# Delta-rule attention: the triangular inverse in 64 by 64 blocks on two array tiles, and the corner block made once

## What is computed

```python
def step(Sm, inp):
    q_, k_, v_, g_, b_ = inp
    Sm = Sm * jnp.exp(g_)[..., None, None]
    kv = jnp.einsum('bhk,bhkv->bhv', k_, Sm)
    delta = (v_ - kv) * b_[..., None]
    Sm = Sm + jnp.einsum('bhk,bhv->bhkv', k_, delta)
    o = jnp.einsum('bhk,bhkv->bhv', q_, Sm)
    return (Sm, o)
_, o = jax.lax.scan(step, S0, (qt, kt, vt, gt, bt))
...
og = o * jax.nn.silu(z)
var = jnp.mean(og * og, axis=-1, keepdims=True)
on = og * jax.lax.rsqrt(var + EPS) * norm_w
return on.reshape(B, S, VAL_DIM) @ w_out
```

## Time and profile before

| | us |
|---|---|
| median of three runs | 6048.98 (6040.39 to 6051.36) |
| span of the profiled execution | 6046.2 |
| delta loop with its last block, in that span | 3160.4 |
| busy in the span: PE / DVE / ACT / POOL | 5221.5 / 3480.2 / 3055.8 / 1178.3 |
| mean granted clock of TensorE over the span | 0.930 |

### The profile page before, as it was taken

One profiled execution on the slowest core, in us unless ns is written; L12 is line 12 of the kernel. 1 busy time (PEld: TensorE's weight loads), 2 busy tenths in 40 slices (PEclk: granted clock), 3 DMA queues, 4 the chain that ended last, 5 costly groups with the idle time before them and its releaser, 6 DMA issues. The chain is left out here.

```text
span 6046.2 us, 91895 instructions
## 1 busy us (share of the span) xinstructions
PE 5221.5 (86%) x32318; PEld 3893.8 (64%) x32318; DVE 3480.2 (58%) x6531; ACT 3055.8 (51%) x8923; POOL 1178.3 (19%) x1352
## 2 busy tenths in 40 slices
PE   5799999999989999989999699899998597399969
PEld 4477777877877778877887555555555354255545
DVE  3466666676666667666766566555552554543331
ACT  2466666666656666666666344344441244325421
POOL 0222222322222222222232100011110321002210
PEclk7799999999999999999999799899999798688879
DMA  2000000000000000000000100100000100000000
GB/s 85 19 19 17 13 19 19 18 17 17 19 19 13 17 19 19 17 14 19 22 19 13 46 1 1 65 1 0 0 0 20 27 1 13 21 1 1 1 21 14
DMA packets 51094, 103.57 MB, mean 17 GB/s; under 512 B 12848, under 2 KB 20176, under 8 KB 49520
## 3 DMA queue, kind: packets, MB, share of 16 engines
q1 hardware_dynamic: 50672, 98.07, 5.4%
HBM read 90.43 MB, written 5.52 MB: 16 GB/s over the span
## 5 line engine op out<-in xcount | busy, mean ns | idle before, releaser
L896 ACT ACTIVATE dh_pb<-bank 64x128 f32<-64x128 f32 x3072 | 831.4, 271 | 272.5 <-PE bank L670 239.3
L684 PE MATMUL bank<-dh_cw,dh_pb 128*128 128x128 f32 x5120 | 701.5, 281 | 113.0 <-ACT dh_pb L896 111.4
L684 PEld LDWEIGHTS bank<-dh_cw,dh_pb 128*128 128x128 f32 x5120 | 635.5, 193 | 191.1 <-ACT dh_pb L896 164.4
L1034 DVE SCALAR_TENSOR_TENSOR dh_kq<-bank,dh_conv_kq,dh_kq 128x511 f32<-128x511 f32 (+2 forms) x408 | 305.4, 749 | 184.8 <-ACT dh_kq L853 173.6
L902 ACT ACTIVATE dh_cw<-bank 128x256 f32<-128x256 f32 x640 | 244.9, 385 | 255.1 <-PE bank L684 247.9
L621 PE MATMUL bank<-hT,dh_w_kq 128*128 128x512 f32 x544 | 276.7, 633 | 83.2 <-DVE dh_kq L1034 75.3
L1034 DVE SCALAR_TENSOR_TENSOR dh_v<-bank,dh_conv_v,dh_v 128x511 f32<-128x511 f32 (+2 forms) x384 | 284.2, 747 | 91.3 <-ACT dh_v L853 82.2
L1797 PE MATMUL bank<-moe_h_split,moe_w 128*128 128x512 bf16 x1200 | 277.1, 381 | 14.6 <-PEq L89 14.6
L633 PE MATMUL bank<-dh_w_vz,hT 128*128 128x256 f32 x1024 | 245.5, 383 | 22.0 <-ACT dh_zs L864 22.0
L1128 DVE TENSOR_TENSOR dh_zz<-dh_zz,bank 128x512 f32<-128x512 f32 x130 | 89.2, 686 | 283.0 <-PE bank L597 281.1
L621 PE MATMUL bank<-hT,dh_w_vz 128*128 128x512 f32 x512 | 242.5, 596 | 8.6 <-DVE dh_v L1034 8.6
(11 more groups left out here) (416 smaller groups left out, 12170.8 us busy)
## 6 DMA issues: line engine op xcount, KB each, us to landing
dh_rates<-delta_rates SPq DMA_DIRECT2D x130, 256.0 KB, 3.6
dh_w_vz<-in_L_wvz SPq DMA_DIRECT2D x17, 512.0 KB, 3.3
mod_w<-in_L_wmod SPq DMA_DIRECT2D x4, 1536.0 KB, 7.0
dh_w_kq<-in_L_wkq SPq DMA_DIRECT2D x18, 256.0 KB, 2.6
dh_wo<-in_L_wo SPq DMA_DIRECT2D x16, 256.0 KB, 4.2
moe_w<-in_L_w13T SPq DMA_DIRECT2D x1, 3200.0 KB, 15.7
later_gates<-mod_gate SPq DMA_DIRECT2D x3, 1024.0 KB, 4.0
gate<-later_gates SPq DMA_DIRECT2D x6, 512.0 KB, 3.4
```

The lines of the kernel that those rows point to most:

```text
L684: last = pe.matmul(square(j)[:, b, :, :], pb[j][:, b, :], src[:, :, b, :], start=True, stop=True)
L896: last = act.activation(out[half, :, o, half], src[halves[o], :, half], ACT.Copy)
L1034: dve.scalar_tensor_tensor(y, pj_bank(n)[:, 0:S - i], taps(n)[:, TAPS - 1 - i:TAPS - i], y, ALU.mult, ALU.add).then_inc(s["v_cs" if i < TA ...
```

## The change

The powers now live in 64 by 64 tiles of the array. Each of the two diagonal blocks of a matrix has its own tile: rows 0 to 63 of the array with columns 0 to 63, and rows 64 to 127 with columns 64 to 127. Calls alternate between the two tiles, then between heads, then sequences. Both a power and its transpose are carried along, so that nothing is transposed in the steps: `flip` turns the first power by a product with the identity; `next_power` (five times) makes the next power from the two; `next_turned` (five) makes the next turned power and the next summand of the turned sum; `inverse` makes the last factor's product, in both orders. The corner block of the inverse is then made once, by `corner_left` (on the tile from the first rows to the last columns) and `corner` (back), and stands in `ttb`. With it `z_prod` alone solves the system: `w_prod`, `w_copy`, `x_prod` and `zeta` are gone. On ACT, `keep_power`, `keep_turned`, `first_block`, `diagonal`, `left_copy` and `corner_copy` take the place of `power` and `power_c`; `qk_copy` on ACT copies k q^T without a mask in place of `qk_mask` on DVE. On DVE, `grow` stays, `last_factor` (L1146) is new, `inverse` and `zeta` are gone.

All recurrence products now share one bank a head (`R_BANK`), where before `B_AUX` was a third. The order of the stages is written anew on PE, ACT and DVE; on POOL `off_diagonal` waits for `corner_left` of the stage before and no longer for w.

```diff
+    def flip(pe, t):
+        for j in HEADS:
+            after(pe, hs[j]["v_u"], t)
+            after(pe, hs[j]["a_u12"], t)
+            for b in range(NB):
+                for p in halves:
+                    last = pe.matmul(pow_bank(j)[p, b, :], c0[j][p, b, :], turn[j][p, EYE, b, :], start=True, stop=True)
...
-        for b in range(NB):
-            last = pe.matmul(square(j)[:, b, :, :], pb[j][:, b, :], src[:, :, b, :], start=True, stop=True)
+        for b in range(NB):
+            for j in HEADS:
+                for p in range(2):
+                    last = pe.matmul(pow_bank(j)[target(j, p), b, :], turn[j][halves[p], CT, b, :], power(i, j)[halves[p], b, :],
+                                     start=True, stop=True)
...
+    def next_turned(pe, t, i):
...
+                    if i < 4:
+                        out, moved = turn_bank(j)[target(j, p), b, :, :], turn[j][halves[p], MOVED[i], b, :]
+                    else:
+                        out, moved = turn_bank(j)[target(j, p), b, T_AT[i], :], turn[j][halves[p], TS[i], b, :]
+                    last = pe.matmul(out, power(i, j)[halves[p], b, :], moved, start=True, stop=True)
...
+    def corner_left(pe, t):
+        for j in HEADS:
+            pe.wait_ge(hs[j]["a_t11"], t + 1)
+            pe.wait_ge(hs[j]["p_nt"], t + 1)
+            for b in range(NB):
+                last = pe.matmul(turn_bank(j)[HI, b, 0, :], off[j][LO, b, :], c_even[j][LO, b, :], start=True, stop=True)
...
+    def corner(pe, t):
...
+                last = pe.matmul(pow_bank(j)[LO, b, :], off[j][HI, b, :], ttb[j][HI, b, HI], start=True, stop=True)
...
-    def w_prod(pe, t, j):
...
-    def x_prod(pe, t, j):
...
     def tensor_stage(pe, t):
...
+        next_power(pe, t, 4)
+        next_turned(pe, t, 4)
+        if a:
+            for j in HEADS: ku(pe, t, j)
...
+        inverse(pe, t)
+        kk_prod(pe, t)
+        qk_prod(pe, t)
+        if a == 1: project(pe, q, 11)
+        if a == 2: project_z(pe, q, 4)
+        corner_left(pe, t)
+        for j in HEADS: y_turn(pe, t, j)
+        if a == 0: project(pe, q, 7)
+        if a == 2: project_z(pe, q, 5)
+        corner(pe, t)
+        for j in HEADS: w_out(pe, t, j)
...
     def vector_stage(dve, t):
...
-        kk_mask(dve, t)
-        for j in HEADS: normed(dve, t, j)
-        for j in HEADS: grow(dve, t, 5, j)
-        qk_mask(dve, t)
-        for j in HEADS: decay(dve, t, j)
-        for j in HEADS: start_power(dve, t, j)
-        inverse(dve, t, 0)
-        collect(dve, t)
-        inverse(dve, t, 1)
+        if a == 0: convolve(dve, q, 5)
+        for j in HEADS: decay(dve, t, j)
+        kk_mask(dve, t)
+        for j in HEADS: start_power(dve, t, j)
+        for j in HEADS: normed(dve, t, j)
+        if a == 0:
+            convolve(dve, q, 6)
+            convolve(dve, q, 7)
+        if a == 1: convolve(dve, q, 11)
+        collect(dve, t)
```

More of the change, by code:

```diff
@@ L657, in qk_prod @@
     def qk_prod(pe, t):
-        pe.wait_ge(s["v_kk"], order(t) + 1)
+        rec_free(pe, t, 1)
         par, c = next_par(t), next_chunk(t)
[L660 to L682, removed]
-        for b in range(NB):
-            last = pe.matmul(square(j)[:, b, :, :], pb[j][:, b, :], src[:, :, b, :], start=True, stop=True)
-        last.then_inc(h["t_ct"], 1)
+        each(pe, R_BANK[1], lambda b: key(par, c, b), lambda b: query(par, c, b)).then_inc(s["t_qk"], 1)
@@ new lines, in inverse @@
+    def inverse(pe, t):
+        for j in HEADS:
+            pe.wait_ge(hs[j]["v_w"], t + 1)
+            pe.wait_ge(hs[j]["v_t"], 5 * t + 5)
+        for b in range(NB):
+            for j in HEADS:
+                at = LO
+                last = pe.matmul(turn_bank(j)[LO, b, 0, :], c_odd[j][at, b, :], turn[j][at, TS[5], b, :], start=True, stop=True)
+        last.then_inc(s["t_t11"], 1)
+        for b in range(NB):
+            for j in HEADS:
+                for p in range(2):
+                    last = pe.matmul(pow_bank(j)[target(j, p), b, :], turn[j][halves[p], TS[5], b, :], c_odd[j][halves[p], b, :],
+                                     start=True, stop=True)
+        last.then_inc(s["t_inv"], 1)
@@ new lines, in tensor_stage @@
+        flip(pe, t)
+        if a == 0: project(pe, q, 0)
+        if a == 1: project_z(pe, q, 0)
+        if a == 2: project(pe, q, 12)
+        if a == 3: project_z(pe, q, 6)
+        for j in HEADS: v_turn(pe, t, j)
+        next_power(pe, t, 0)
+        next_turned(pe, t, 0)
+        if old:
+            for j in HEADS: ks(pe, t, j)
+        if a == 0: project(pe, q, 1)
+        if a == 1: project(pe, q, 8)
+        if a == 2: project(pe, q, 13)
+        if a == 3: project_z(pe, q, 7)
+        next_power(pe, t, 1)
@@ new lines, in tensor_stage @@
+        next_turned(pe, t, 1)
+        for j in HEADS: z_prod(pe, t, j)
+        if a == 0: project(pe, q, 2)
+        if a == 1: project_z(pe, q, 1)
+        if a == 2: turn_kq(pe, q, 0)
+        if a == 3: turn_kq(pe, q, 4)
+        next_power(pe, t, 2)
+        next_turned(pe, t, 2)
+        if old:
+            for j in HEADS: qs(pe, t, j)
+        if a == 0: project(pe, q, 3)
+        if a == 1: project(pe, q, 9)
+        if a == 2: project(pe, q, 14)
+        if a == 3: turn_kq(pe, q, 5)
@@ new lines, in tensor_stage @@
+        next_power(pe, t, 3)
+        next_turned(pe, t, 3)
+        for j in HEADS: pu(pe, t, j)
+        if a == 0: project(pe, q, 4)
+        if a == 1:
+            project_z(pe, q, 2)
+            project(pe, q, 10)
+        if a == 2:
+            turn_kq(pe, q, 1)
+            project(pe, q, 15)
+        if a == 3: turn_kq(pe, q, 6)
+        next_power(pe, t, 4)
[3 more added lines that the diff above has]
+        if a == 0:
+            project(pe, q, 5)
+            project(pe, q, 6)
@@ new lines, in scalar_stage @@
+        if a == 3: squares(act, q, 6)
+        for j in HEADS: mean_sq(act, t, j)
+        if a == 0:
+            silu(act, q, 3)
+            tap(act, q, 5)
+            silu(act, q, 4)
+            tap(act, q, 6)
+        if a == 1:
+            silu(act, q, 10)
+            silu_z(act, q, 3)
+        if a == 2:
+            squares(act, q, 2)
+            squares(act, q, 3)
+        if a == 3: squares(act, q, 7)
+        for j in HEADS: first_block(act, t, j)
+        for j in HEADS: diagonal(act, t, j)
@@ L1184, in vector_stage @@
         old = rec_chunk(t) > 0
-        if old:
-            for j in HEADS: rhs(dve, t, j)
-        grow(dve, t, 1, 0)
         if a == 0: convolve(dve, q, 0)
@@ L1481, in _ @@
         def _(dve):
-            for f in (rhs, zeta, q_state, output, normed):
+            for f in (rhs, q_state, output, normed):
                 for j in HEADS: f(dve, 0, j)
```

548 lines of the change are left out of this document (232 added, 316 removed).

## The result

The changed kernel takes 6164.51 us (median of 4 runs, 6158.78 to 6165.86) against 6044.68 us of the kernel before on the same chip: a ratio of 1.0195, with a 95% interval of 1.018 to 1.0209. The forecast was 6110 us within 5930 to 6390: the direction held, the size was about twice what was said. The profiled span is 6156.8 us, 110.6 longer than before.

The account below looks back on a forecast made before the run. TensorE was taken to bound the loop. Per set, 103.1 + 70.5 + 12.0 + 10.5 = 196.1 us against 193.64: +40 over 16 sets; with clock +27 and last block -6, forecast 6110 us, range 5930 to 6390.

Parts of the forecast that it names:

- kept work: PE's work in the delta loop that the change leaves in place: 103.1 us in a set of four stages.
- tiled work: New 64x64 products on PE, two tiles side by side: 17.6 us a stage, 70.5 a set.
- switches: PE going from full to tiled products and back, nine times a stage at 0.33 us: 12.0 us a set.
- rivals 2 and 3: Tiles not side by side, about 7070 us; 64 columns as dear as 128, about 6700; chance 0.05 each.
- Rival 4: The clock also falls in tiled stretches, since half of the array is in use: about 6500 us; chance 0.07.
- The old waits: Waits and hand-overs in the loop before, some 23 us a set; most were to go.
- Rival 1: Faster: waits shrink to some 4 us a set as DVE arrives earlier, no clock falls; 5962 us, chance 0.29.
- The new wait: y_turn on PE waits for DVE's normed, now behind decay and start_power: 1 to 4 us in a = 0, 2, 3.
- The table: PE against DVE from pu's end to y_turn, giving normed waits; with hand-overs, 1.4 for squares and 1.5 elsewhere, 10.5 us.
- The clock: Low clock after one of three new waits in each loop set: 16 x 1.7 = 27 us, bounds 0 and 80.
- the prediction's own sign: The forecast is wrong if the loop's granted clock leaves 0.99 by more than 0.01.
- The last block: The block after the loop loses w, x and zeta: about -6 us.

Follow-up runs that it names:

- e1: Changed kernel with normed and kk_mask put back ahead of decay and start_power on DVE: 5948.4 us, ratio 0.9846 to the kernel before.
- e2: Changed kernel with useless transposes on PE while y_turn waits for normed: 6079.47 us, ratio 1.0064 to the kernel before.
- e3: Changed kernel with head 1's tiled products on the two other tiles, its inverse wrong, for time alone: 5927.3 us, ratio 0.9809.
- e5: e1 with head 1 on the two other tiles and a right inverse, its sum multiplied by power plus identity: 5696.3 us, ratio 0.9436.

## Why the prediction was right in direction and short in size

**PE's work: right.** The forecast had 103.1 us of kept work, 70.5 of tiled work and 12.0 of switches in a set, 185.6. e1, whose waits are 1.2 and 1.0 us, takes 187.0. The stage a = 1 of the changed kernel, which has no wait, takes 46.46 us against 26.1 + 20.6 = 46.7 forecast; if its tiled records take the 17.6 us of the forecast, 2.8 are left for nine switches, 0.31 each. A next_power group took 0.98 us (forecast 1.0), a next_turned group 1.85 (1.8). The statement that the tiles do the work of squares, transposes, w and x at about the same price on PE, and that the switches come on top, holds: PE's floor rose by some 14 us a set. That settles rivals 2 and 3: 16 records a tile in 0.98 us are 0.061 each with the switch included, neither one after another nor as dear as 128 columns. The 60 cycles a matmul of the Trainium skill (TensorEngine Tiling (Array Packing), Instruction Overhead) are not seen on top of it here. Rival 4 fell with e2 and with the stage a = 1: the clock is 1.00 through tiled products.

**The old waits: right.** The 23 us of before shrank, and with `normed` in its old place (e1) some 2.3 us are left. That gain is larger than the rise of the floor, so the change with its new order on DVE undone is faster. Rival 1 had the waits shrink this far with the order as it stood; the point that it called decisive, normed's end against corner_left's end, went against it.

**The new wait: right in place and order, in its total partly by luck.** The table said 1.1, 0, 2.0 and 3.8 us for the four stages and 10.5 for all waits of a set; measured were 1.7, 0, 2.0 and 5.2, and 8.9 + 1.2 = 10.1 in all. y_turn's waits are 2.0 longer than said, and the 1.5 "elsewhere" and the hand-overs, which did not come, make up for it. a = 3 is 1.4 longer; start_power at 4.1 us in place of 3.26 makes 0.9 of that. Nor need POOL work "on the same data": `injected`, beside it for half of the time, reads and writes other tiles (ident, dh_R, dh_inj).

**The clock: the step that failed.** "I let one of the three new waits of a set do this: 16 x 1.7 = 27" took the price from one short fall and let the clock fall once a set. e2 measured 79 us. In 12 of the 16 stages a = 3 the clock stayed at 0.50 for 10.2 us, three times as long as in the earlier trace rows, and in the other four for 6.8; it fell for 3.4 us in 14 of the stages a = 0 too, and in 6 of the stages a = 2. By the prediction's own sign (the loop's clock no more than 0.01 off 0.99) this term was wrong: the clock is 0.96. The bound of 80 was in the forecast, but the value was taken well below its middle. The wait of a = 3 is a stretch with no work at all, where the earlier trace rows have one with half. A nearer row was in the trace of the kernel before, in the block after the loop, where y_turn and w_out also follow a wait for normed:

```profile
3386.54 1.97 PE L602 MATMUL bank<-ident,dh_yy 128*128 128x128 f32 x8 [6.68 <-DVE dh_yy L1172]
3388.34 5.57 PE L759 MATMUL bank<-dh_wo_gated,dh_ww 128*128 128x256 f32 x16
```

Start to start y_turn's eight transposes take 1.80 us there, where four take 0.44, and the row of w_out is 5.57 long, where it is 3.62 there: 2.9 us lost, not 1.7. The rest of the sum held together: without its clock term the forecast is +34 us, and e2, which has the wait and not the fall, measured +39 (some 8 of them its own transposes).

**The last block: right in sign, too large.** From its first transposes to its end it takes 27.4 us where it took 31.0: about 3.6 us less, not 6.

Taken together, by ratios: the tiles and the corner in e1's order give -93 us, the place of `normed` +132, the clock behind it +79 (up to 87, see e2); the sum is +118. That the four tiles of e3 and e5 were open to this kernel was not seen.

## What to carry to other kernels

When an inner computation is rewritten, look at what else was reordered around it: here one line's place on an engine that is busy 60% of the time cost more than the rewriting gained. Price a wait of the matmul engine together with the clock behind it, and by several rows: here low stretches of 3.4 to 10.2 us followed such waits, and one short row made the term a third of what it was. And where two of the four 64x64 tiles are in use, ask whether the other two can have work of their own: giving them the second head (e5 against e1) took off 4.1% of the time of the kernel before, some 248 us, more than all the rest.

## What was not expected of the hardware

- Four 64x64 tiles took 0.51 us for 32 records of 64 columns where two took 0.98 (e3): also tiles on the same rows run side by side. The Trainium skill (TensorEngine Tiling (Array Packing), Key Properties) says that different tiles work independently; these rows agree.
- The clock, once it had fallen in an idle stretch of 5.2 us, stayed low for 10.2 us, while y_turn, corner and w_out followed each other with little idle time. In a later layer of the kernel before, an idle stretch of 4.62 us was followed by only 3.42 us at 0.50, so the length of the idle stretch alone does not tell how long the clock stays low. What ended it is not told by these runs.
- start_power's four instructions took 1.74 us alone and 4.14 beside POOL, 2.4 times as long, on 64 partitions by 256 elements each.
